# Two products of a chain in a perceiver kernel, from fp32 to three fp32r products each

## The reference

```python
x = x + xattn(layernorm(x), ctx, ctx)      # softmax(q k^T / 16) v, then @ Wo + bo
x = x + attn(layernorm(x))                 # causal; Q, K, V from x with Wq, Wk, Wv
x = x + ffn(layernorm(x))                  # x + shared_out + routed_out, gelu experts
# within xattn:
value = v @ Wv + bv
out = jnp.einsum('bqk,bkd->bqd', attn, value)
return out @ Wo + bo
# within attn:
V = jnp.einsum('bsd,od->bso', x, Wv) + bv
Z = jnp.einsum('bqs,bso->bqo', attn, V)
```

## Time and profile before

| | us |
|---|---|
| median of 3 runs (lowest to highest) | 253.06 (252.71 to 253.97) |
| the profiled execution | 252.87 |
| its span in the profile | 251.1 |
| PE busy in the span | 242.7 |
| DVE busy | 153.5 |
| ACT busy | 135.5 |

### The profile page before, as it was taken

The page is one execution under the profiler, slowest core; times in us unless marked ns, Lnnn a source line. Parts: engine busy times, 40 slices in busy tenths (PEclk is TensorE's granted clock), DMA queues, the critical chain, the costliest instruction groups (busy, mean ns, idle before and its releaser), DMA issues.

```text
span 251.1 us, 5120 instructions
## 1 busy us (share of the span) xinstructions
PE 242.7 (97%) x1908; PEld 209.4 (83%) x1908; DVE 153.5 (61%) x371; ACT 135.5 (54%) x265; POOL 50.2 (20%) x81
## 2 busy tenths in 40 slices
PE   8799998999999999999999999999999999999994
PEld 8656645366367599999998999999999999999994
DVE  0833244453654897788849246666667666667683
ACT  2225205152152778886867256666666666666641
POOL 5100000000100200230587002112122111126700
PEclk9999999999999999999999999999999999999999
DMA  7999999999999999950157448999999999920142
GB/s 253 423 432 397 423 407 431 377 404 425 356 379 341 323 315 426 422 238 0 45 169 295 105 130 287 364 373 364 360 354 349 371 346 360 347 117 21 54 137 84
DMA packets 14254, 74.12 MB, mean 295 GB/s; under 512 B 1524, under 2 KB 8956, under 8 KB 9884
## 3 DMA queue, kind: packets, MB, share of 16 engines
q1 hardware_dynamic: 12700, 70.59, 74.9%
q0 software_dynamic: 1008, 2.76, 2.9%
q10 hardware_dynamic: 528, 0.52, 0.6%
HBM read 67.56 MB, written 6.32 MB: 294 GB/s over the span
## 4 chain that ended last, share of the span: by engine, by line
PE 71%; DMA 15%; DVE 4%; POOL 3%; issue 2%; SPq 2%; ACT 2%; DVEq 0%; POOLq 0%; ACTq 0%
PE psum L512 61%; DMA rows<-rows_dram 11%; PE psum L760 4%; POOL slot_x_dram L479 3%; DMA slot_x_dram<-second,rows_of 3%; PE psum L601 2%; PE psum L778 1%; DMA xrow<-slot_x_dram 1%; ACT prob L879 1%; DVE cmax L1083 1%; PE psum L821 1%; SPq L337 1%; PE psum L650 1%; PE psum L692 0%; DVE xs L1107 0%
## 5 line engine op out<-in xcount | busy, mean ns | idle before, releaser
L512 PE MATMUL psum<-xrowT,ring 128*128 128x128 f32 x480 | 58.3, 275 | 0.0
L512 PEld LDWEIGHTS psum<-xrowT,ring 128*128 128x128 f32 x480 | 56.2, 192 | 0.0
L1303 DVE TENSOR_TENSOR dlo<-ring,dhi 128x1024 fp32r<-128x1024 f32 x30 | 38.3, 1280 | 3.8 <-ACT dhi L962 3.8
L1322 DVE TENSOR_TENSOR slot_hlo<-slot_h,slot_hhi 128x512 fp32r<-128x512 f32 x30 | 20.8, 693 | 30.0 <-ACT slot_hhi L990 30.0
L988 ACT ACTIVATE slot_h<-psum 128x512 f32<-128x512 f32 x30 | 18.0, 600 | 35.5 <-PE psum L512 35.5
L512 PE MATMUL psum<-dhi,slot_hhi 128*128 128x256 f32 x120 | 36.3, 302 | 0.1
L512 PE MATMUL psum<-dhi,slot_hlo 128*128 128x256 f32 x120 | 33.8, 282 | 0.0
L512 PE MATMUL psum<-dlo,slot_hhi 128*128 128x256 f32 x120 | 33.8, 282 | 0.0
L962 ACT ACTIVATE dhi<-ring 128x1024 fp32r<-128x1024 f32 x30 | 31.1, 1040 | 0.0
L504 POOL DMA_INDIRECT results_dram<-y_rows,result_row x13 | 14.6, 1119 | 72.6 <-DMA results_dram<-y_rows,result_row 56.2
L512 PE MATMUL psum<-xh,parted 128*128 128x256 f32 x128 | 26.8, 286 | 0.0
(11 more groups left out here) (195 smaller groups left out, 398.4 us busy)
## 6 DMA issues: line engine op xcount, KB each, us to landing
ring<-experts_dram SPq DMA_DIRECT2D x15, 2048.0 KB, 8.5
ctx<-ctx_dram SPq DMA_DIRECT2D x4, 3072.0 KB, 24.5
ctxT_start<-ctxT_start_dram SPq DMA_DIRECT2D x4, 2048.0 KB, 19.0
ctxT_rest<-ctxT_rest_dram SPq DMA_DIRECT2D x4, 1154.0 KB, 21.4
raw<-experts_dram SPq DMA_DIRECT2D x2, 2048.0 KB, 15.4
slot_x_dram<-empty_row SPq DMA_DIRECT2D x1, 1935.0 KB, 16.2
xrow<-slot_x_dram SPq DMA_DIRECT2D x15, 129.0 KB, 7.4
squares<-squares_dram SPq DMA_DIRECT2D x1, 1285.0 KB, 14.2
```

What stands on the lines that cost most here:

```text
L512: return pe.matmul(out, lhsT, rhs, start=first, stop=last)
L1303: dve.tensor_tensor(dlo[b % 2][:, steps, :], ring[b][:, steps, C * P:STEP_W], dhi[b % 2][:, steps, :].bitcast(F32), ALU.subtract).then_inc ...
L1322: dve.tensor_tensor(slot_hlo[:, half, :], slot_h[:, half, :], slot_hhi[:, half, :].bitcast(F32), ALU.subtract).then_inc(slot_hlo_ready, 1)
```

## The change

proj and v are computed in parts. New tiles hold a high and a low part each: `wvo_parts` and `awv_parts` for the two matrices, `mixT` (now with a part index) and `xn2T_parts` for the moving side of the chain. PE runs six fp32r matmuls of 128 x 256 where it ran two in fp32 (`in_parts`). The parts of the matrices are made once, by a step `chain_weights` that stands ahead of the first exp of pair 1: two copies of 128 x 512 on ACT and two subtractions on DVE.

`mixT` is now made by two engines: ACT copies the high part from PSUM, then DVE subtracts. `xn2T` stays, since tq and sc use it; ACT makes a high part from it right behind its copy, and DVE a low part at the place of tq in ORDER. The dot product `c2_dot`, which stood at that place, goes to the place of xn2T. v now waits for the low part (`xn2T_lo`).

The new tiles lie where the first six matrices of `squares` lie, which are dead by then. SP loads `ring3` over that space, so the load of ring buffer 3 (and with it those of buffers 0 and 1 behind it in SP's list) now waits for the last proj and the last v of the four pairs.

```diff
+            with ExitStack() as chain_phase:
+                wvo_parts = sb("wvo_parts", [P, 2, C, D], F32R, chain_phase)
+                awv_parts = sb("awv_parts", [P, 2, C, D], F32R, chain_phase)
+                mixT = sb("mixT", [P, 2, C, P], F32R, chain_phase)
+                xn2T_parts = sb("xn2T_parts", [P, 2, C, P], F32R, chain_phase)
...
             sp.wait_ge(pv_ps, T)
             load(2, 2)
+            sp.wait_ge(proj_ps, T)
+            sp.wait_ge(v_ps, T)
             load(3, 3)
             sp.wait_ge(wlo_ready, J)
             load(0, 0)
...
+            def in_parts(out, left, right):
+                parts = [(c, lp, rp) for lp, rp in ((0, 0), (0, 1), (1, 0)) for c in range(C)]
+                for c, lp, rp in parts:
+                    ins = mm(out, left[:, lp, c, :], right[:, rp, c, :], (c, lp, rp) == parts[0],
+                             (c, lp, rp) == parts[-1])
+                return ins
...
-                for c in range(C):
-                    ins = mm(bank(V_BANKS[t], 0, D), xn2T[:, c, :], squares[:, AWVT, c, 0:D], c == 0, c == C - 1)
-                ins.then_inc(v_ps, 1)
+                if t == 0:
+                    pe.wait_ge(chain_lo, 2)
+                pe.wait_ge(xn2T_lo, t + 1)
+                in_parts(bank(V_BANKS[t], 0, D), xn2T_parts, awv_parts).then_inc(v_ps, 1)
...
+            def mixT_high(t):
+                act.wait_ge(mixT_ps, t + 1)
+                act.activation(mixT[:, 0, :, :].rearrange("p c n -> p (c n)"), bank(chain_bank(t), 0, D), ACT.Copy
+                               ).then_inc(mixT_hi, 1)
...
+                act.wait_ge(xn2T_sb, t + 1)
+                if t >= 1:
+                    act.wait_ge(v_ps, t)
+                act.activation(xn2T_parts[:, 0, :, :], xn2T[:, :, :], ACT.Copy).then_inc(xn2T_hi, 1)
...
-            def mixT_copy(t):
-                dve.wait_ge(mixT_ps, t + 1)
-                dve.tensor_copy(mixT[:, :, :].rearrange("p c n -> p (c n)"), bank(chain_bank(t), 0, D)
-                                ).then_inc(mixT_sb, 1)
+            def mixT_low(t):
+                dve.wait_ge(mixT_hi, t + 1)
+                dve.tensor_tensor(mixT[:, 1, :, :].rearrange("p c n -> p (c n)"), bank(chain_bank(t), 0, D),
+                                  mixT[:, 0, :, :].bitcast(F32).rearrange("p c n -> p (c n)"), ALU.subtract
+                                  ).then_inc(mixT_sb, 1)
...
-                    "tq": c2_dot, "sc": softmax2, "v": v_copy, "z": x2_add, "xl": split_x,
+                    "xn2T": c2_dot, "tq": xn2T_low, "sc": softmax2, "v": v_copy, "z": x2_add, "xl": split_x,
```

More of the change, by code:

```diff
@@ L76, in plan @@
         order += [("S", t + 1, 0), ("S", t + 1, 1), *having(c, "xn2T"), *having(late, "xn3T", "xl"),
-                  ("S", t + 1, 2), *having(c, "tq"), ("S", t + 1, 3), ("exp", t + 1, 0), ("exp", t + 1, 1),
-                  *([("W", t, 0, 3)] if t else []), *having(c, "sc", "v", "exp2"),
+                  ("S", t + 1, 2), *having(c, "tq"), ("S", t + 1, 3), *([] if t else [("chain_weights", )]),
+                  ("exp", t + 1, 0), ("exp", t + 1, 1), *([("W", t, 0, 3)] if t else []), *having(c, "sc", "v", "exp2"),
                   ("exp", t + 1, 2), ("exp", t + 1, 3), ("W", t, 3 if t else 4, KT)]
@@ L189, in build @@
                            sb(f"ctxT{i}_rest", [P, 2, C, KV - 2 * BANK], F32, phase1))
-            squares = sb("squares", [P, 7, C, D + 1], F32, phase1)
+            with ExitStack() as fold_phase:
+                squares = sb("squares", [P, 7, C, D + 1], F32, fold_phase)
+            with ExitStack() as chain_phase:
[3 more added lines that the diff above has]
+                xn2T_parts = sb("xn2T_parts", [P, 2, C, P], F32R, chain_phase)
+            sb("room_for_squares", [P, 7, C, D + 1], F32, phase1)
             aq = sb("aq", [P, C, D], F32, phase1)
@@ L201, in build @@
             mix = sb("mix", [P, D], F32, phase1)
-            mixT = sb("mixT", [P, C, P], F32, phase1)
             xn2T = sb("xn2T", [P, C, P], F32, phase1)
@@ L278, in build @@
         pv_ps, mix_ready, mixT_ps, mixT_sb = sem("pv_ps"), sem("mix_ready"), sem("mixT_ps"), sem("mixT_sb")
+        mixT_hi, xn2T_hi, xn2T_lo = sem("mixT_hi"), sem("xn2T_hi"), sem("xn2T_lo")
+        chain_hi, chain_lo = sem("chain_hi"), sem("chain_lo")
         proj_ps, x1_ready, xn2_ready, xn2T_ps, xn2T_sb = (
@@ L641, in chain_proj @@
                 if t == 0:
-                    pe.wait_ge(fold_act, 2)
-                for c in range(C):
-                    ins = mm(bank(chain_bank(t), 0, D), mixT[:, c, :], wvo[:, c, :], c == 0, c == C - 1)
-                ins.then_inc(proj_ps, 1)
+                    pe.wait_ge(chain_lo, 1)
+                in_parts(bank(chain_bank(t), 0, D), mixT, wvo_parts).then_inc(proj_ps, 1)
             def chain_xn2T(t):
@@ L891, in probT_copy, with chain_weights @@
                 ins.then_inc(probT_act, 1)
+            def chain_weights():
+                act.wait_ge(fold_act, 3)
+                act.wait_ge(fold_ps, 5)
+                act.activation(wvo_parts[:, 0, :, :], wvo[:, :, :], ACT.Copy).then_inc(chain_hi, 1)
+                act.activation(awv_parts[:, 0, :, :], squares[:, AWVT, :, 0:D], ACT.Copy).then_inc(chain_hi, 1)
+            def mixT_high(t):
+                act.wait_ge(mixT_ps, t + 1)
+                act.activation(mixT[:, 0, :, :].rearrange("p c n -> p (c n)"), bank(chain_bank(t), 0, D), ACT.Copy
+                               ).then_inc(mixT_hi, 1)
             def xn2T_copy(t):
@@ L975, in _ @@
                            ).then_inc(fold_act, 1)
-            mine = {"T": probT_copy, "exp": exps, "xn2T": xn2T_copy, "tq": tq_copy, "exp2": exp2,
+            mine = {"T": probT_copy, "exp": exps, "chain_weights": chain_weights, "mixT": mixT_high, "xn2T": xn2T_copy, "tq": tq_copy, "exp2": exp2,
                     "probT": prob2T_copy, "xn3T": xn3T_copy, "split": split,
@@ L1122, in mix_scale, with chain_weights, xn2T_low @@
                 dve.tensor_scalar(mix[:, :], bank(PO, 0, D), linv[:, 0:1], None, ALU.mult).then_inc(mix_ready, 1)
-            def mixT_copy(t):
-                dve.wait_ge(mixT_ps, t + 1)
-                dve.tensor_copy(mixT[:, :, :].rearrange("p c n -> p (c n)"), bank(chain_bank(t), 0, D)
-                                ).then_inc(mixT_sb, 1)
+            def chain_weights():
+                dve.wait_ge(chain_hi, 1)
+                dve.tensor_tensor(wvo_parts[:, 1, :, :], wvo[:, :, :], wvo_parts[:, 0, :, :].bitcast(F32), ALU.subtract
+                                  ).then_inc(chain_lo, 1)
+                dve.wait_ge(chain_hi, 2)
+                dve.tensor_tensor(awv_parts[:, 1, :, :], squares[:, AWVT, :, 0:D], awv_parts[:, 0, :, :].bitcast(F32),
+                                  ALU.subtract).then_inc(chain_lo, 1)
+            def mixT_low(t):
[3 more added lines that the diff above has]
+                                  ).then_inc(mixT_sb, 1)
+            def xn2T_low(t):
+                dve.wait_ge(xn2T_hi, t + 1)
+                dve.tensor_tensor(xn2T_parts[:, 1, :, :], xn2T[:, :, :], xn2T_parts[:, 0, :, :].bitcast(F32),
+                                  ALU.subtract).then_inc(xn2T_lo, 1)
             def x1_add(t):
@@ L1304, in split_down @@
                                   dhi[b % 2][:, steps, :].bitcast(F32), ALU.subtract).then_inc(dlo_ready, 1)
-            mine = {"T": probT_copy, "bias_folds": bias_folds, "S": max_chunk, "W": weigh, "mixT": mixT_copy, "proj": x1_stats,
+            mine = {"T": probT_copy, "bias_folds": bias_folds, "S": max_chunk, "W": weigh,
+                    "chain_weights": chain_weights, "mixT": mixT_low, "proj": x1_stats,
                     "norm2": norm2, "norm3": norm3,
-                    "tq": c2_dot, "sc": softmax2, "v": v_copy, "z": x2_add, "xl": split_x,
+                    "xn2T": c2_dot, "tq": xn2T_low, "sc": softmax2, "v": v_copy, "z": x2_add, "xl": split_x,
                     "split": lambda q: split_low(q, q % J, q // J % 2),
```

1 line of the change is left out of this document (removed).

## The result

The changed kernel takes 254.46 us in the median of its runs, the kernel before 252.95 us in the runs beside it (252.38 at the least). The ratio is 1.0053 with a 95% interval of 1.0041 to 1.0066, so the change costs 1.0 to 1.7 us, 1.34 by the ratio. (One run of each kernel, 403.31 us after and 851.46 us before, stands far above the rest and is not in the ratio.) The forecast was +0.5 us, within 0.5% of no change; the time lies in the range (252.0 to 254.5) at its upper edge, and 0.9 us above the likeliest value (253.6). The profiled execution of the changed kernel took 254.82 us, its span is 252.6 us.

A forecast was written before the change was run, and what follows sets the result against it. PE, busy 97% of the span, was taken as the bound, reaching the first slot together with pair 3's chain. Lateness 1.15 - p less lead G gave +0.53 us on 252.87, with 0.2 for the median 253.6 us; range 252.0 to 254.5.

The forecast's parts named there:

- p: Saving of one proj or v product, six fp32r matmuls for four fp32 records: 0.09 to 0.16 us, 0.12 taken.
- G: As a forecast term: PE's lead up to W of pair 3, five products' saving less 0.1 us, 0.5 us.
- Rival C: The six matmuls cost what passes alone would, saving 0.21 us a product: 253.1 us; chance 0.05.
- The wait at v of pair 2: DVE makes the low part of xn2T from 89.49 to 89.91, so PE waits 0.86 us, until 90.00.
- mixT of pair 3: DVE's low part comes 1.03 us later; proj needn't wait, but PE waits another 0.4 us at the norm's transposes.
- ACT behind it: Four splits move by 1.59 us; ACT's idle times bring it back to PE's 1.03 us at tq of pair 3.
- rival B: ACT doesn't catch up after its high part of mixT of pair 3, scores late: +1.5 us, 254.5; chance 0.15.
- The steps of the engines together: Lateness from the waits at pairs 2 and 3 less the savings, 1.25 - 6p: +0.53 us.
- three hops of 0.1 us: Hops between engines off by 0.1 us at three places, part of the span 253.1 to 254.2 us.
- The sign that failed: Forecast is wrong if W of pair 3 isn't earlier; some 0.5 us earlier was expected.
- The start: chain_weights has cover, ACT idle for 11 us ahead of pair 1's first exp: nothing; without cover 1.3 us.
- The later ring loads: SP issues buffers 3 and 0 at about 102 us, buffer 0 is first read at 131.40: cost nothing.

The follow-up runs named there:

- C: Changed kernel with only proj in parts, v in fp32 and no parts of xn2T: 253.35 us, ratio 1.0022 to the kernel before.
- D: Changed kernel with only v in parts, proj in fp32 and mixT copied by DVE: 253.41 us, ratio 1.0020 to the kernel before.
- A: Changed kernel with DVE's low part of xn2T and the dot product c2_dot exchanged in order: 253.57 us, ratio 1.0021 to the kernel before.
- G: Kernel before with only SP's two new waits ahead of the load of ring buffer 3: 252.85 us, ratio 0.9997.
- H: Kernel before with the changed layout, five new semaphores and SP's two waits, none of the new instructions: 252.92 us, ratio 0.9996.
- I: Changed kernel with A's exchange on DVE, and ACT's high part of mixT of pair 3 behind one split: 253.07 us, ratio 0.9985 to the kernel before.
- B: Changed kernel with DVE instead of ACT making the high part of mixT of pair 3: 254.57 us, ratio 1.0063 to the kernel before.
- K: Changed kernel with the row of biases loaded by ACT right behind x: 254.70 us, ratio 1.0052 to the kernel before.
- L: Version I with the row of biases loaded by ACT right behind x: 253.14 us, ratio 1.0007 to the kernel before.

## Why the prediction held, and where it was off

- **p, the saving of a product.** Forecast 0.09 to 0.16 us, 0.12 taken; measured 0.09 at v of pair 2 (0.78 against 0.87), 0.12 at proj of pair 3 (0.75), and 0.63 us over the five products up to W of pair 3, where I had G = 0.50. C and D each show half of it. The 0.1 us set aside for waits at mixT of pairs 0 to 2 wasn't needed. Rival C, at 0.21 us a product, would have had 1.05 us for the five.
- **The wait at v of pair 2.** Forecast: DVE from 89.49 to 89.91, PE at 90.00. Measured: 89.50 to 89.91, PE at 90.06. Experiment A shows that this order is its cause, and that it costs 0.98 us to tq of pair 3.
- **mixT of pair 3.** ACT waited at the semaphore as described (1.28 us), the low part started at 91.67 (91.58 forecast), proj came without a wait.
- **The step that failed: ACT behind it.** I had compared ACT's lateness with PE only at tq of pair 3, and said that it is caught up there. I overlooked that hid 3 reuses the buffer of hid 0 and so waits for the gelu of unit 0 (`gelu_done`, n >= LEAD in `unit_hidden`). That gelu was at 95.41 instead of 93.74, and hid 3 waited 0.41 us. On the way from the splits to that gelu ACT also has an exp and a table load of 1.28 us, and no idle time that could have taken the lateness up. DVE's norm of pair 3 was 1.06 us late (1.03 forecast), but PE's transposes were 1.38 us late, and tq 1.27 us; so the wait of 0.4 us that I had put ahead of these transposes came at hid 3 instead. This is rival B's mechanism, ACT's lateness reaching PE, at a place I hadn't looked at and at a quarter to a third of a microsecond instead of one.
- **The steps of the engines together**: +0.53 forecast, +0.65 measured. The upper end of that sum was added up 0.1 us too high: 0.71 and three hops of 0.1 us give 254.1, not 254.2.
- **The sign that failed.** I had written that I am wrong if W of pair 3 isn't earlier. By the clock of the trace it isn't (81.35 against 81.34 us), and the first slot came 1.5 us later (142.10 against 140.59) instead of 0.5. The saving ahead of W is there, counted from T of pair 1 (39.06 against 39.69), and the late start hides it.
- **The start, costed at nothing.** I had looked only at whether chain_weights delays the first exp of pair 1. It doesn't: DVE's subtractions run behind the maximum, as forecast. But T of pair 1 is 0.64 us late since the loads land later, and that is the largest part of what I missed (1.34 by the ratio less 0.53, 0.8 us). No row of the kernel before showed it. The rest lies in the fifth stretch: the last scatter lands 7.8 and 8.0 us after its issue in the two profiles of the changed kernel, against 6.7 and 6.8 before. The two chains of work, before and after:

```profile
130.88 6.72 DMA slot_x_dram<-second,rows_of
137.62 2.93 DMA xrow<-slot_x_dram
```

```profile
132.18 7.79 DMA slot_x_dram<-second,rows_of
139.99 2.07 DMA xrow<-slot_x_dram
```

- **The later ring loads**: costed at nothing, and G shows nothing.
- **The size of the range.** The chance of slower by over 0.5% was put at 0.15, and the measured ratio sits right at that bound; the range held, with 0.04 us to spare. That is luck in part: the engines' steps were forecast, but the larger half of the excess came from two groups of DMAs that the sum had at nothing.

Open: why the start's loads land later in programs with the new instructions. Layout and semaphores (H) and the later ring loads (G) are excluded. The first new instructions are ACT's two copies of `chain_weights`, at 27.96 to 29.10 us. The first context load lands at 25.6 to 26.1 us without them and at 25.9 to 26.1 in the changed kernel, C, D and I, all but the same, and the context of pair 1 behind the copies at 30.5 to 31.0 without them and at 31.2 to 31.5 with (30.8 in C, which has one copy). So the copies themselves are a rival that these profiles allow. Against it: in A and B already the first context load lands late (26.6 and 26.5 us), ahead of the copies. No run has the copies alone, or as many instructions without their work.

Open also why the scatter lands 1.1 us later in the changed kernel and in K, but not in A to D, I or L, whose way from the first scatter to the reload is 16.6 to 17.0 us like before (16.7 and 16.8; 17.8 to 18.0 in the changed kernel and K). B runs the same products in parts and has 16.8. This was seen and not tested.

## What to carry to other kernels

A product that is moved to parts saves a little on the matrix engine and puts two more hops, another engine's copy and a subtraction, into the chain ahead of it; in a kernel whose order is written out by hand, where these steps stand in the queues of the two engines decides the sum, and here it made the difference between -0.52 us (I) and +0.65 us in the engines' steps. When an engine is made to wait early, follow everything queued behind it to each consumer, buffers that are reused among them, and not only to the consumer on the chain in hand. Before adding work, look what stands idle just ahead of the new step's place: DVE had a gap of 0.8 us, and with the low part in it (A) the wait at v was gone.

## What the runs showed of the hardware

- A six-matmul fp32r product of 128 x 256 took 0.75 to 0.78 us against 0.87 us for the same product as two fp32 matmuls, at a granted clock of 1.0 (2.4 GHz): 10 to 14% less.
- The start's loads landed at different times by the program, with the same loads, bytes and order of issue: the row of biases let DVE go on at 34.33 to 34.65 us in four profiles without new instructions (before twice, G, H), and at 34.85 to 35.49 us in seven profiles with new instructions from 28 us on.
- The last of eight scatters of 128 rows landed 6.7 and 6.8 us after its issue in the kernel before and 7.8 and 8.0 us in the changed one, with the ring load ahead of it issued 2.4 us earlier in both.
- Behind a standstill of 2.81 us of PE in L, 16 fp32 matmul records of 128 x 512 took 5.18 us at a granted clock of 0.70; behind one of 2.99 us in K they took 3.65 us at 1.00. Such a standstill can cost the clock, and needn't.
